# Block 1's first half normed and routed earlier by ScalarE and GpSimd, with first scores inside block 0's feed-forward

## What is computed

```python
x = x + tanh(g_x[0]) * xattn0(layernorm(x), ctx)  # 16 heads of 64, causal
x = x + tanh(g_f[0]) * moe0(layernorm(x))         # 8 experts + 4 zero experts, top 2, all computed
x = x + tanh(g_x[1]) * xattn1(layernorm(x), ctx)  # 16 heads of 8, biases, no mask
x = x + tanh(g_f[1]) * moe1(layernorm(x))         # 8 routed experts, top 2, + 2 shared ones
# top 2: logits = x @ gate_w + bias; softmax over the two best; every expert is computed, gates weight them
```

## Time and profile before

| | |
|---|---|
| median of 3 runs | 272.99 (272.81 to 273.55) |
| profiled execution | 273.14, its span 271.1, mean granted TensorE clock 0.996 |
| busy share of the span | TensorE 91%, VectorE 70%, ScalarE 41%, GpSimd 26% |
| chain that ended last | TensorE 66%, VectorE 16%, issue 5%, DMA 4%, ScalarE 4%, GpSimd 2% |
| block 0 attention, about | 9 to 122 |
| block 0 feed-forward | 122 to 185 |
| attention 1 | 185 to 232 |
| block 1 feed-forward | 232 to 268 |

### The profile page before, as it was taken

One profiled execution on the slowest core, in us unless ns is written; L12 is line 12 of the kernel. 1 busy time (PEld: TensorE's weight loads), 2 busy tenths in 40 slices (PEclk: granted clock), 3 DMA queues, 4 the chain that ended last, 5 costly groups with the idle time before them and its releaser, 6 DMA issues.

```text
span 271.1 us, 7236 instructions
## 1 busy us (share of the span) xinstructions
PE 247.6 (91%) x2956; PEld 210.0 (77%) x2956; DVE 190.0 (70%) x478; ACT 110.5 (41%) x187; POOL 69.6 (26%) x83
## 2 busy tenths in 40 slices
PE   8879989899999999989999998998798988879992
PEld 3558878788998888769999997997576877757881
DVE  1537798967365989896256586438788998879753
ACT  2565545544441554323134453430636454221220
POOL 2355393445433533340010031001122001111000
PEclk9999999999999999999999999999999999999998
DMA  6519600030000000598499100340052000000011
GB/s 200 188 45 321 175 1 4 2 157 4 0 2 2 1 2 7 87 147 308 189 169 171 49 0 0 118 116 1 2 174 63 2 2 5 0 0 4 8 30 41
DMA packets 14705, 18.98 MB, mean 70 GB/s; under 512 B 2384, under 2 KB 11472, under 8 KB 14544
## 3 DMA queue, kind: packets, MB, share of 16 engines
q1 hardware_dynamic: 14528, 18.26, 25.6%
q10 hardware_dynamic: 144, 0.26, 0.5%
HBM read 13.80 MB, written 4.72 MB: 68 GB/s over the span
## 4 chain that ended last, share of the span: by engine, by line
PE 66%; DVE 16%; issue 5%; DMA 4%; ACT 4%; POOL 2%; SPq 1%; DVEq 0%
PE OC L1130 9%; PE MB L1090 5%; PE MB L980 5%; PE SP L1051 5%; PE OC L1073 5%; PE TP L1060 4%; PE MB L982 4%; PE MB L981 4%; PE TP L1243 3%; PE MB L1202 2%; PE MB L1206 2%; PE OC L1079 2%; DMA w_raw<-in_w 2%; PE SP L982 2%; PE SP L980 2%
## 5 line engine op out<-in xcount | busy, mean ns | idle before, releaser
L398 POOL TENSOR_TENSOR S_sb<-S_sb,nmax 128x512 f32<-128x512 f32 x32 | 33.2, 1039 | 38.9 <-DVE nmax L701 38.9
L798 DVE SCALAR_TENSOR_TENSOR x_sb<-OC,gate,x_sb 128x128 f32<-128x128 f32 x64 | 18.0, 345 | 26.8 <-PE OC L1130 26.8
L1130 PEld LDWEIGHTS OC<-f_w,hid 128*128 128x128 f32 x256 | 30.9, 192 | 1.4
L692 DVE TENSOR_TENSOR S_sb<-SP,maskb 128x512 f32<-128x512 f32 x32 | 21.9, 686 | 13.5 <-PE SP L1051 13.3
L1130 PE MATMUL OC<-f_w,hid 128*128 128x128 f32 x256 | 31.0, 275 | 0.0
L701 DVE TENSOR_REDUCE nmax<-S_sb 128x4 f32<-128x512 f32 x32 | 22.0, 686 | 1.1
L507 ACT ACTIVATE PT<-TP 128x512 f32<-128x512 f32 x32 | 19.0, 593 | 7.8 <-PE TP L1060 7.7
L1060 PE MATMUL TP<-id_sb,S_sb 128*128 128x128 f32 x128 | 19.6, 275 | 2.4 <-POOL S_sb L398 2.4
L368 POOL TENSOR_SCALAR var_eps<-mv 128x4 f32<-128x4 f32 x8 | 2.0, 245 | 70.9 <-DVE mv L646 70.9
L1073 PE MATMUL OC<-PT,arena_f 128*32 128x128 f32 x512 | 17.6, 275 | 2.3 <-issue 1.7
L1060 PEld LDWEIGHTS TP<-id_sb,S_sb 128*128 128x128 f32 x128 | 14.9, 141 | 5.6 <-POOL S_sb L398 3.9
(11 more groups left out here) (187 smaller groups left out, 582.5 us busy)
## 6 DMA issues: line engine op xcount, KB each, us to landing
arena_f<-in_zeros SPq DMA_DIRECT2D x1, 2048.0 KB, 14.5
w_raw<-in_w SPq DMA_DIRECT2D x4, 384.0 KB, 4.0
k_dram<-f_r SPq DMA_DIRECT2D x3, 512.0 KB, 13.9
...
```

The lines of the kernel that those rows point to most:

```text
L398: g.tensor_tensor(S_sb[:, b], S_sb[:, b], nmax[:, b].unsqueeze(2).to_broadcast([P, H4, P]), ALU.add).then_inc(shifted, 1)
L692: v.tensor_tensor(S_sb[:, b].rearrange("p (r a) k -> p r a k", r=2), SP[:, :, 2 * P * b:2 * P * (b + 1)].rearrange("p r (a k) -> p r a k", ...
L1130: ins = mm(OC[:, n % 2, batch(t)], hid[:, n % 2, c, batch(t)], f0_w2[:, e, c, :], start=(c == 0), stop=(c == 1))
```

## The change

- Block 0's feed-forward: half 1 is transposed, routed and gated one expert sooner (hooks 4, 5, 6 instead of 5, 6, 7); half 0's statistics stay at 7. `queries1(0)` stands right behind `hidden0(11)`. `scores1(0, 0)`, `scores1(0, 1)`, `maxima1(0)` and `scores1(1, 0)` are issued inside the loop, at 13, 14 and 15; the first two and the first turned group use the two ring banks (`SPARE`), so that the three areas stay with the experts. `max1(0, .)` and `shift1(0)` follow on VectorE at 12, 13 and 14.
- Queries: half 0 still goes through DRAM, with the rows already stored, and is loaded in one transfer of 128 partitions for each two sequences. Half 1 does not: `spread_queries(i)` selects and places its parts by two matmuls with 0/1 weights, and ScalarE copies the result into `q1s` (`place_queries`). Weights' columns are permuted on the host to fit. Keys are loaded in one transfer; `row_dram`, its eight loads and the `col_sel` load are gone (`row_of` takes its place).
- Attention 1: `outputs1` is copied to SBUF by ScalarE (`copy_outputs`), VectorE transposes the sums, inverts 16 numbers a row and transposes back, GpSimd multiplies. Fillers: 20 and 6 instead of 24, 16, 16 and 6; none before the gates.
- Tail: `output1(0, .)` one sequence sooner (b = 6). Its residual is scaled on ScalarE and added on GpSimd; half 0's and half 1's norm is made by ScalarE as `rstd * x + offset`, the offset from GpSimd; half 0's flat copy is ScalarE's and its low part GpSimd's. `xn_transposes(3, 0)` and `logits(1, 0)` stand one output group earlier. `route_best(1, 0)` stands before the last `normalise1`, `xn_transposes(3, 1)`, `logits(1, 1)`, and `gates_turn(1)` one step later.

The core of the diff:

```diff
+SPARE = [("s", 0, 0), ("s", 0, 1), ("t", 0, 0)]
+AREAS = [("s", 1, 0), ("s", 1, 1), ("t", 0, 1)]
...
-            def place_heads(dst, dram, tok, moved):
-                for j in range(4):
-                    sp.dma_start(dst[32 * j:32 * j + 24, :, tok].bitcast(F32),
-                                 dram.rearrange("(j i) r t -> j r i t", j=4)[j]).then_inc(moved, 16)
+                sp.dma_start(dram.rearrange("i (j r) t -> (i j) r t", j=4)[:, DH1 * c:DH1 * (c + 1), :], src.bitcast(F32)
+                             ).then_inc(sent, 16)
+
+            def place_heads(dst, dram, moved):
+                sp.dma_start(dst.bitcast(F32), dram.rearrange("i p t -> p i t")).then_inc(moved, 16)
...
-            for h in range(2):
-                sp.wait_ge(q1_his, h + 1)
-                send_heads(q_dram[h], 0, q1_hi[:], q_sent[h])
-                send_heads(q_dram[h], 1, q1_hi[:], q_sent[h])
-                sp.wait_ge(q1_los, h + 1)
-                send_heads(q_dram[h], 2, q1_lo[:], q_sent[h])
-                sp.wait_ge(q_sent[h], 48)
-                for w in range(2):
-                    tok = slice(2 * P * w, 2 * P * (w + 1))
-                    place_heads(q1s[:, :, half(h)][:, :, tok], q_dram[h][:, :, tok], slice(0, 2 * P), q_moved[2 * h + w])
+            sp.wait_ge(q1_his, 1)
+            send_heads(q_dram, 0, q1_hi[:], q_sent)
+            send_heads(q_dram, 1, q1_hi[:], q_sent)
+            sp.wait_ge(q1_los, 1)
+            send_heads(q_dram, 2, q1_lo[:], q_sent)
+            sp.wait_ge(q_sent, 48)
+            for w in range(2):
+                tok = slice(2 * P * w, 2 * P * (w + 1))
+                place_heads(q1s[:, :, tok], q_dram[:, :, tok], q_moved[w])
...
+            def offset_of(h):
+                pool.wait_ge(stat, nth(3, h))
+                link(pool, "pool", g.tensor_scalar(offset[:, 0, seqs(h)], mv[:, seqs(h), 0], -1.0, None, ALU.mult))
+                rstd_of(3, h)
+                pool.wait_ge(rstds, nth(3, h))
+                g.tensor_tensor(offset[:, 1, seqs(h)], offset[:, 0, seqs(h)], rstd[:, seqs(h)], ALU.mult).then_inc(offset_set, 1)
+
+            def residual(w):
+                pool.wait_ge(scaled, w + 1)
+                g.tensor_tensor(x_sb[:, 2 * w:2 * w + 2, :], x_sb[:, 2 * w:2 * w + 2, :], xn[:, 2 * w:2 * w + 2, :], ALU.add
+                                ).then_inc(res, 1)
+
+            def xnT_lo_copy():
+                pool.wait_ge(flat_, nth(1, 0))
+                g.tensor_tensor(xnT_lo[:, half(0)], xnT[:], xnT_hi[:, half(0)].bitcast(F32), ALU.subtract).then_inc(lo_, 1)
+
+            def normalise1(b):
+                pool.wait_ge(o_sum1, 3 * (b + 1))
+                g.tensor_tensor(oT1[:, batch(b)], o_sb[:, b % 2, 0:P], R1[:, b % 2], ALU.mult).then_inc(o_done1, 1)
...
+                     3: [lambda: split_f1(2), lambda: split_f1(3)], 6: [lambda: residual(0), lambda: residual(1)],
+                     7: [lambda: offset_of(0)]}
             for b in range(B):
                 for hook in hooks.get(b, ()):
                     hook()
+                if b > 1:
+                    normalise1(b - 2)
+            xnT_lo_copy()
+            normalise1(B - 2)
             best_difference(1, 0)
-            rstd_of(3, 1)
+            offset_of(1)
...
+            def place_queries(i):
+                name = ("p", i)
+                wait_full(act, name)
+                sc.activation(q1s[:, i, half(1)], ring(name), ACT.Copy).then_inc(placed, 1)
...
+            def scale_output(w):
+                name = ("y1", 0, w)
+                wait_full(act, name)
+                sc.activation(xn[:, 2 * w:2 * w + 2, :], ring(name)[:, 0:2 * P].rearrange("p (b d) -> p b d", b=2), ACT.Copy,
+                              scale=tanh_g[:, 1:2]).then_inc(scaled, 1)
+
+            def normed(h):
+                act.wait_ge(offset_set, h + 1)
+                for b in range(HB * h, HB * (h + 1)):
+                    sc.activation(xn[:, b, :], x_sb[:, b, :], ACT.Identity, bias=offset[:, 1, b:b + 1], scale=rstd[:, b:b + 1]
+                                  ).then_inc(normed_, 1)
+
+            def xnT_flat_copy(h):
+                sc.activation(xnT[:], ring(("t", 3, h)), ACT.Copy).then_inc(flat_, 1)
+
+            def copy_outputs(b):
+                name = ("o", b)
+                wait_full(act, name)
+                if b > 1:
+                    act.wait_ge(o_done1, b - 1)
+                sc.activation(o_sb[:, b % 2], ring(name)[:, 0:2 * P], ACT.Copy).then_inc(o_copied, 1)
...
+            exp1(0, 0)
+            exp1(0, 1)
+            xnT_hi_copy(2, 1)
+            queries1(1)
+            exp1(1, 0)
+            exp1(1, 1)
+            for i in range(4):
+                place_queries(i)
+            hooks = {2: [lambda: split_f1(0), lambda: split_f1(1)], 3: [lambda: split_f1(2), lambda: split_f1(3)],
+                     6: [lambda: scale_output(0), lambda: scale_output(1)]}
+            for b in range(2, B):
                 for hook in hooks.get(b, ()):
                     hook()
+                copy_outputs(b - 2)
+                if b == B - 1:
+                    normed(0)
                 exp1(b, 0)
-                exp1(b, 1)
+                if b < B - 1:
+                    exp1(b, 1)
             xnT_hi_copy(3, 0)
-            hooks = {1: [lambda: gates_hi(0)], 2: [lambda: xnT_hi_copy(3, 1)], 5: [lambda: gates_hi(1)]}
+            xnT_flat_copy(0)
+            exp1(B - 1, 1)
+            copy_outputs(B - 2)
+            copy_outputs(B - 1)
+            hooks = {1: [lambda: gates_hi(0)], 2: [lambda: normed(1), lambda: xnT_hi_copy(3, 1)], 6: [lambda: gates_hi(1)]}
...
+                dve.wait_ge(o_copied, b + 1)
+                v.transpose(sumT[:], o_sb[:, b % 2, P:2 * P].rearrange("p (c r) -> p c r", r=32)).then_inc(o_sum1, 1)
+                dve.wait_ge(o_sum1, 3 * b + 1)
+                v.reciprocal(rsum1[:], sumT[:, :, 0:4]).then_inc(o_sum1, 1)
+                dve.wait_ge(o_sum1, 3 * b + 2)
+                if b > 1:
+                    dve.wait_ge(o_done1, b - 1)
+                v.transpose(R1[:, b % 2].rearrange("p (c i d) -> p c i d", c=4, i=4),
+                            rsum1[:].unsqueeze(3).to_broadcast([P, 4, 4, DH1])).then_inc(o_sum1, 1)
+                if b == B - 1:
+                    dve.wait_ge(o_sum1, 3 * (b + 1))
                     dve.wait_ge(o_done1, b)
-                v.reciprocal(R1[:], ring(name)[:, P:2 * P]).then_inc(o_sum1, 1)
-                dve.wait_ge(o_sum1, b + 1)
-                ins = v.tensor_tensor(oT1[:, batch(b)], ring(name)[:, 0:P], R1[:], ALU.mult)
-                ins.then_inc(o_done1, 1)
+                    v.tensor_tensor(oT1[:, batch(b)], o_sb[:, b % 2, 0:P], R1[:, b % 2], ALU.mult).then_inc(o_done1, 1)
...
+                     2: [lambda: normed(1, 1)], 3: [lambda: xnT_lo_copy(1, 1)],
+                     4: [lambda: route_best(0, 1, (0,))], 5: [lambda: route_best(0, 1, (1,))],
+                     6: [lambda: route_gates(0, 1)], 7: [lambda: stats_of_sum(0)], 8: [lambda: normed(2, 0)],
+                     9: [lambda: xnT_lo_copy(2, 0), lambda: queries1(0)], 12: [lambda: max1(0, 0)],
+                     13: [lambda: max1(0, 1)], 14: [lambda: shift1(0)]}
...
+            max1(1, 0)
             normed(2, 1)
-            early = {1: [lambda: queries1(1)]}
-            mid = {0: [lambda: xnT_lo_copy(2, 1)], 7: [lambda: residual(1, 0, 0), lambda: residual(1, 0, 1),
-                                                       lambda: stats_after(3, 0)]}
-            late = {7: [lambda: normed(3, 0)]}
-            for b in range(B):
+            max1(1, 1)
+            xnT_lo_copy(2, 1)
+            shift1(1)
+            max1(2, 0)
+            queries1(1)
+            max1(2, 1)
+            for b in range(2, B):
                 shift1(b)
-                for hook in early.get(b, ()):
-                    hook()
                 if b + 1 < B:
                     max1(b + 1, 0)
                     max1(b + 1, 1)
-                for hook in mid.get(b, ()):
-                    hook()
-                if b > 1:
-                    normalise1(b - 2)
-                for hook in late.get(b, ()):
-                    hook()
+                normalise1(b - 2)
+                if b == B - 2:
+                    stats_after(3, 0)
             normalise1(B - 2)
-            xnT_lo_copy(3, 0)
+            route_best(1, 0)
             normalise1(B - 1)
-            route_best(1, 0)
-            residual(1, 1, 0)
-            residual(1, 1, 1)
-            hooks = {0: [lambda: route_gates(1, 0), lambda: stats_after(3, 1), lambda: gates_lo(0), lambda: normed(3, 1)], 1: [lambda: xnT_lo_copy(3, 1)],
-                     2: [lambda: route_best(1, 1)], 3: [lambda: route_gates(1, 1)], 4: [lambda: gates_lo(1)],
-                     5: [lambda: finish(0, 0), lambda: finish(0, 1)]}
+            route_gates(1, 0)
```

(71 more changed lines are left out.)

204 lines of the change are left out of this document (103 added, 101 removed).

## The result

The changed kernel takes 278.81 us in the median (277.33 to 280.1, 4 runs), the kernel before 273.27 beside it; the ratio is 1.0187, with a 95% interval of 1.0148 to 1.0226. The forecast was 272.1 with a range of 270.4 to 274.0. The change makes this kernel slower, by some 1.5 to 2.3%, and the range doesn't hold the time.

What follows compares the result with a forecast made beforehand. TensorE, busy nine tenths of the span, was taken as the full engine, with its waits deciding. Terms +0.82 - 2.70 - 0.80 + 1.20 + 0.6 = -0.9 took the median of 272.99 to 272.1 us; range 270.4 to 274.0.

Steps and rivals of the forecast that it cites:

- E: Start of VectorE's last expert addition in block 0: 184.47 before, forecast 185.29 plus a stall S.
- E to the exponential of sequence 2: Step from the last expert to the sequence loop: 16.4 instead of 19.10, -2.70.
- The tail: From `outputs1(3)` on: `hidden1(0)` after 16.55 and the last `expert1` after 50.85 instead of 49.65, +1.20.
- Rival 3: Clock falls to 1.2 GHz in tail waits of about 1.75 or 2.3: +2.5, 274.6 us; chance 0.16.
- the term of the clock: TensorE's granted clock stays full throughout, adding nothing to the time.
- The exponentials of sequence 0: On ScalarE after the last expert addition: start at 0.6, so fillers and exponentials no longer stand between.
- S: TensorE's wait before `scores1(0, 0)` for the query load in block 0's loop: 0 to 1.8, taken as 0.6.
- rival 1: No stall, and half 1 costs the tail +0.5 instead of +1.20: 270.8 us; chance 0.24.
- the 0.82: Block 0's expert loop moves E by +0.82, stall S not included.
- Sequence 3: Attention loop: its exponential follows sequence 2's by a period of 4.25 instead of 5.05, -0.80.
- The row sums' turn: Attention loop on VectorE: two transposes and a small reciprocal, 0.92, replace 0.98 + 0.21; worth nothing to the 4.25 cycle.
- the case of the lock: GpSimd and VectorE sharing a port pair: each new GpSimd step some 0.5 longer; 0 to +0.5, taken as 0.

Runs made afterwards that it cites:

- gap_fill: all_three with 28 instead of 20 fillers after the turned scores of sequence 0; 273.50 us, ratio 0.9992 to the kernel before.
- spread_fill: Changed kernel with 8 fillers between the second and third `spread_queries`; 277.04 us, ratio 1.0126.
- tail_fill: Changed kernel with 20 fillers before `xn_transposes(3, 0)` and 18 before `expert1(1)` in the tail's two waits; 276.08 us, ratio 1.0103.
- all_three: Changed kernel with the edits of early_table, tail_fill and spread_fill together; 273.77 us, ratio 1.0036.
- tail_bare1: norm_back with half 1's statistics ahead of `gates_lo(0)`, without the 12 fillers before half 0's transposes in the tail; 272.01 us, ratio 0.9935.
- early_table: Changed kernel with a one-column exponential right after the last SiLU, loading the table early; 278.95 us. Its rival: that wait is hidden by statistics and norm.
- before_bare: Kernel before without the 24 and 10 fillers that the change took out; 278.13 us, ratio 1.0099.
- one_wait: gap_fill without the early exponential, the first exponential of sequence 0 waiting for one bank of turned scores instead of two; 273.25 us, ratio 0.9990.
- norm_back: gap_fill with both halves' last norm on VectorE again and 12 instead of 20 fillers before half 0's transposes; 271.25 us, ratio 0.9913.
- tail_bare2: norm_back with half 1's statistics ahead of `gates_lo(0)`, without the 18 fillers before `expert1(1)`; 270.53 us, ratio 0.9899.

## Why the prediction was wrong

**Where 4.4 of the loss lies.** After against gap_fill, in the profiled runs: E comes 0.21 earlier; E to the exponential of sequence 2 takes 19.65 against 16.69, +2.96; from there to the turned scores behind `outputs1(3)` both take 12.06 (217.37 and 214.62); from there to the last `expert1` 53.71 against 52.05, +1.66; the end is the same. Sum +4.41, and the spans differ by 275.5 - 271.1 = 4.4. Of the 2.96, all but 0.06 is the two falls of the head: spread_fill, with the late table load and the full clock, takes 16.75. The tail's 1.66 is its two falls (tail_fill, with the full clock there, takes 51.96 like gap_fill), and nearly all of it (18.75 against 17.31 at `hidden1(0)`, 1.44) is there after the first of them. The profiled run is the shortest of the four; the others have spans 1.3 to 2.8 longer at mean clocks of 0.960 to 0.965 against its 0.971, and no trace shows where.

**Rival 3 was the one that happened, and it was held too small.** It had a chance of 0.16 and a price for one fall, of 2.5. The mechanism and both places in the tail were right. The step that failed is the term of the clock, which the forecast put at nothing ("full clock throughout"). Its reason was "It decides where a wait comes up to the 1.8 of the end". By that sentence itself the second wait, forecast at 2.3, was long enough, and the first, forecast at 1.75, all but was; they measured 2.27 and 2.34, and in the profiled run the clock fell 1.8 to 1.9 into each. Nor is 1.8 a bound: it is the one fall in the trace of before, at its end. In the head the clock fell 0.5 into a wait of 1.25, and in all_three 2.0 after one of 1.04; a wait of 1.44 was enough in seven runs of ten (tail_bare1). The kernel before, on the other side, has waits of 1.19 and 1.29 at full clock in its profiled run:

```profile
196.77 1.92 PE L987 MATMUL MB<-warm_sb 128*128 128x256 bf16 x16 [1.29 <-DVE q_lo L827]
```

The price hangs on how long a fall lasts: 2.9 for the two of 3.4 in the head of after, about 1.7 for one in tail_bare1, 2.4 for one of 6.8 in all_three (19.05 against 16.69), 4.8 for one of 13.6 in early_table (21.52). The kernel after has four. The rival also looked at the tail alone. In the head the change takes 24 fillers from one wait and puts 20 behind a ScalarE instruction, and the prediction named no wait there; before_bare measures what the removed ones held. The rule of the Trainium skill (TensorE: Matmul & The Clock Gate, how the oscillation bites), that idle gaps put the array back to the low clock, agrees with these runs in its direction. It is stated there for longer gaps than the waits of 1.0 to 2.3 here, and two falls came while TensorE worked, so the measurement decides. With 46 fillers in three gaps and the table load moved, the changed kernel takes 5 less (all_three).

**The exponentials of sequence 0.** "The exponentials of sequence 0 start at 0.6, for its scores, maxima and shift are behind": they start at 2.0 after E. The table was the wrong one after the last Silu. Since these scores now lie in the two banks of `MB`, the exponential has one more wait, and the load stands behind one of them (186.37, idle 4.58 before it), so the idle time doesn't hide it. With an early exponential (gap_fill) or one wait fewer (one_wait) the start is E + 0.7, and the step holds. At full clock the late start costs this kernel nothing (spread_fill), as the rival of early_table says; it matters by the wait of 1.25 that it gives TensorE. `wait_area` is in the diff; that a wait can hold a load back had to be seen from the order of the instructions.

**S.** No stall: `scores1(0, 0)` started without waiting in the traces of after and gap_fill, as rival 1 has it. E came at 185.66, or 185.87 in gap_fill, where the forecast with its 0.6 had 185.89 and without it 185.29. All twelve changed kernels are alike up to there, and their E lies between 185.34 and 185.91, 185.65 in the median; so the loop itself costs 0.4 more than the 0.82, give or take 0.3. The two errors hide each other, by luck.

**E to the exponential of sequence 2**: 16.69 at full clock against 16.4. **Sequence 3** follows 4.26 later, and the loop has its period of 4.25: right. The row sums' turn, GpSimd's product of 0.46 and the copy on ScalarE cost nothing, as said. GpSimd's new steps took 0.46 and 1.42 (two residuals), no longer than forecast. VectorE's instructions beside them read at most one operand from SBUF (maxima, shift, transposes), so the case of the lock didn't arise, and these rows don't test it.

**The tail** failed by 1.2 at full clock: 52.05 against 50.85. The offset is there when it should be, 10.27 after the turned scores (10.3). But the four activations take 1.65, where the prediction took 1.0 from a pitch of 0.25: a copy's time for an activation with scale and bias of its own per partition. `hidden1(0)` comes at 17.31 (16.55), `expert1(1)` at 27.72 (27.1), the transposes of half 1 at 30.02, 1.2 late, and that goes through to the end. "Moving it gains nothing on this way" should have been "costs": norm_back gets 2.2 by moving it back.

**The end** is 4.43 behind the last `expert1` where the profiled run of before has 5.03. "What follows it (finish, store) is not changed" put this at nothing. The two traces with the old tail have 5.03 and 5.13 (before, before_bare), and eleven of the twelve with the changed one 4.41 to 4.50; tail_bare2 alone has 5.66. The issue of the last two stores takes 0.89 (gap_fill) instead of 1.15, and the rest is behind it:

```profile
267.78 1.15 SPq L354 DMA_DIRECT2D out_x<-xn  x2
268.38 0.89 SPq L370 DMA_DIRECT2D out_x<-xn  x2
```

So the 0.6 most likely comes with the change; what in it shortens the stores was not tested.

**The sum at full clock**: E -0.02, to sequence 2 +0.29, tail +1.20, end -0.60, together +0.87, against a forecast span of 270.2 and one of 271.1 in gap_fill. So the range would have held it, and "within 0.3%" too, helped by the end that nobody forecast: without its clock falls the change does next to nothing to the time (a ratio of 0.9992; median spans of 271.0 against the 270.8 of those runs of before that have the full clock).

**What stays open**: why the clock fell at 201.7 with short waits alone, and why waits of nearly the same length bring a fall in some runs and not in others. spread_fill was made for the first question and can't answer it, since the fall of 188 was missing there too; no run was made for the second.
